# A mixture of experts on one core: seven wide products per pair, four of them summed in one PSUM bank, two weight sums made by adding DMAs

## What is computed

```python
h = relu(einsum('bi,eio->beo', x, eW1) + eb1)       # 512 x 1024 by 1024 x 1024, 8 experts
h = relu(einsum('beh,eho->beo', h, eW2) + eb2)      # to 512
expert_out = einsum('beh,eho->beo', h, eW3) + eb3   # to 256
gates = softmax(einsum('bi,tie->bte', x, gW) + gb, axis=-1)      # 2 tasks
tin = einsum('bte,bed->btd', gates, expert_out)
th = relu(einsum('btd,tdh->bth', tin, tW1) + tb1)
th = relu(einsum('bth,tho->bto', th, tW2) + tb2)
out = sigmoid(einsum('bth,tho->bto', th, tW3) + tb3)[..., 0]
```

## Time and profile before

| | us |
|---|---|
| median of three runs (579.86 to 580.24) | 580.05 |
| the profiled execution | 580.12 |
| its span, first to last instruction | 578.5 |
| TensorE busy | 572.7 |
| VectorE busy | 462.6 |
| ScalarE busy | 265.3 |
| GpSimd busy | 44.1 |

### The profile page before, as it was taken

One profiled execution on the slowest core, in us unless ns is written; L12 is line 12 of the kernel. 1 busy time (PEld: TensorE's weight loads), 2 busy tenths in 40 slices (PEclk: granted clock), 3 DMA queues, 4 the chain that ended last, 5 costly groups with the idle time before them and its releaser, 6 DMA issues.

```text
span 578.5 us, 9216 instructions
## 1 busy us (share of the span) xinstructions
PE 572.7 (99%) x3315; PEld 501.7 (87%) x3315; DVE 462.6 (80%) x590; ACT 265.3 (46%) x336; POOL 44.1 (8%) x46
## 2 busy tenths in 40 slices
PE   8999999999999999999999999999999999999998
PEld 5788899988999889988999889988999889998776
DVE  6955489985998769895898859987699859988492
ACT  3545274524545164333654255351654346533553
POOL 0000100030000300012000300003000210004000
PEclk9999999999999999999999999999999999999999
DMA  8340622243131514215223422415131241235000
GB/s 311 137 145 1 229 101 74 76 173 116 73 117 64 188 66 145 73 60 230 73 73 108 161 93 73 145 36 220 42 137 73 97 193 73 73 131 167 29 0 2
DMA packets 23277, 63.27 MB, mean 109 GB/s; under 512 B 1617, under 2 KB 6865, under 8 KB 19682
## 3 DMA queue, kind: packets, MB, share of 16 engines
q1 hardware_dynamic: 21906, 58.64, 28.3%
q0 software_dynamic: 1216, 4.23, 2.0%
q10 hardware_dynamic: 144, 0.26, 0.1%
HBM read 63.08 MB, written 0.04 MB: 109 GB/s over the span
## 4 chain that ended last, share of the span: by engine, by line
PE 96%; DMA 1%; ACT 1%; DVE 1%; issue 0%; SPq 0%; ACTq 0%
PE psum L280 25%; PE psum L282 25%; PE psum L281 25%; PE psum L425 13%; PE psum L427 7%; DMA w_raw<-eW_first 1%; DVE w_lo L787 0%; PE psum L487 0%; ACT w_hi L742 0%; ACT w_hi L586 0%; ACT scratch L777 0%; PE psum L572 0%; SPq L300 0%; DVE scratch L1079 0%; ACT h_hi L680 0%
## 5 line engine op out<-in xcount | busy, mean ns | idle before, releaser
L280 PE MATMUL psum<-h_hi,w_hi 128*128 128x512 f32 (+1 forms) x340 | 131.6, 387 | 0.8 <-DVE h_lo L798 0.8
L282 PE MATMUL psum<-h_hi,w_lo 128*128 128x512 f32 (+1 forms) x340 | 131.6, 387 | 0.0
L281 PE MATMUL psum<-h_lo,w_hi 128*128 128x512 f32 (+1 forms) x340 | 131.6, 387 | 0.0
L787 DVE TENSOR_TENSOR w_lo<-w_raw,w_hi 128x1024 fp32r<-128x1024 f32 (+1 forms) x79 | 111.2, 1426 | 3.2 <-ACT w_hi L742 1.7
L798 DVE SCALAR_TENSOR_TENSOR h_lo<-scratch,h_hi 128x512 fp32r<-128x512 f32 (+1 forms) x68 | 61.7, 909 | 50.1 <-ACT scratch L681 37.8
L282 PE MATMUL psum<-t_both,w_lo 128*128 128x256 f32 x336 | 95.1, 283 | 0.0
L281 PE MATMUL psum<-t_both,w_hi 128*128 128x256 f32 x336 | 95.0, 283 | 0.0
L280 PE MATMUL psum<-t_both,w_hi 128*128 128x256 f32 x336 | 95.0, 283 | 0.0
L627 ACT ACTIVATE w_hi<-w_raw 128x1536 fp32r<-128x1536 f32 x28 | 41.8, 1494 | 90.4 <-PE psum L282 46.2
L280 PEld LDWEIGHTS psum<-h_hi,w_hi 128*128 128x128 f32 x340 | 63.9, 188 | 14.2 <-DVE h_lo L798 1.2
L282 PEld LDWEIGHTS psum<-h_hi,w_lo 128*128 128x128 f32 x340 | 63.8, 188 | 13.0
(11 more groups left out here) (101 smaller groups left out, 798.6 us busy)
## 6 DMA issues: line engine op xcount, KB each, us to landing
w_raw<-eW_pairs SPq DMA_DIRECT2D x28, 1024.0 KB, 4.8
w_raw<-eW SPq DMA_DIRECT2D x40, 512.0 KB, 3.7
scratch<-gates_dram POOLq DMA_DIRECT2D x8, 512.0 KB, 3.9
w_raw<-eW_first SPq DMA_DIRECT2D x7, 512.0 KB, 6.3
w_raw<-tW SPq DMA_DIRECT2D x4, 512.0 KB, 3.4
scratch<-xT SPq DMA_DIRECT2D x7, 256.0 KB, 6.2
w_raw<-eW_first SPq DMA_DIRECT2D x2, 256.0 KB, 4.0
scratch<-xT ACTq DMA_DIRECT2D x1, 256.0 KB, 3.4
```

Of the source, the lines that this page charges most:

```text
L280: pe.matmul(bank, weights_hi, moving_hi, start=first, stop=False)
L281: pe.matmul(bank, weights_hi, moving_lo, start=False, stop=False)
L282: return pe.matmul(bank, weights_lo, moving_hi, start=False, stop=last)
L787: dve.tensor_tensor(wide(w_lo, slots), raw, wide(w_hi, slots).bitcast(F32), ALU.subtract).then_inc(slot_ready, 1)
```

## The change

All seven products are wide, in the order P1, P2, P5, P6, P4 of the pair before, P3, P7; P4 of the last pair stands between layer 3 and layer 2. P1, P6, P7 and P4 of a pair are summed one upon the other in one bank (N_BANK); ScalarE reads the bank after P1 (`n1_take`), after P6 (`n2_take`) and after P4 (`c21_take`), VectorE after P7 (`c22_sum`). P5 and P3 share another bank (Q_BANK), read by ScalarE between them (`p5_take`) and by VectorE behind P3 (`c12_sum`). P2 has a bank of its own. TensorE waits for each such reading before it adds to the bank. VectorE folds the halves (`upper_fold`, `lower_fold`, `c21_fold`). The weight blocks of a pair lie in the order A22, A11, A12, A21; their sums and those of x have other signs. S2 and S4 are made on VectorE as before. S1 and S3 are made by transfers from GpSimd's queue that add a block from DRAM to one that SP has loaded: per pair, SP loads 768 KB of blocks, 256 KB for S3 and 256 KB of A22, and GpSimd adds 256 KB twice. The splits of a pair are four groups: G1 (three slots), G2 (one), G3 (two), G4 (one). GpSimd's loop is unrolled. The four gated outputs are `gate_output(e, n)` at places of their own. Buffers in SBUF are laid out anew and the units of W3, W2 and the tower weights are others.

```diff
-PRODUCTS = [((0, 10), True, "x", 1, 0),
-            ((4, 14), False, "x", 0, 0),
...
+N_BANK, Q_BANK, P2_BANK = [2, 6, 3, 2], [0, 1, 0, 1], [3, 4, 5, 4]
+PRODUCTS = {"P1": (N_BANK, "x", 0, 0, True, False), "P2": (P2_BANK, "x", 1, 0, True, True), "P5": (Q_BANK, "t", 0, 0, True, False),
+            "P6": (N_BANK, "t", 1, 1, False, False), "P4": (N_BANK, "t", 1, 0, False, True), "P3": (Q_BANK, "x", 1, 1, False, True),
+            "P7": (N_BANK, "t", 0, 1, False, False)}
+SPLIT_ORDER = [("G1", 0), ("G2", 0), ("G3", 0), ("G1", 1), ("G4", 0), ("G2", 1), ("G3", 1), ("G4", 1),
+               ("G1", 2), ("G2", 2), ("G3", 2), ("G1", 3), ("G2", 3), ("G4", 2), ("G3", 3), ("W3",), ("G4", 3),
+               ("W2", 0), ("W2", 1), ("W2", 2), ("W2", 3)]
...
# SP, per expert
+                sp.wait_ge(slot_ready, splits(e) - 2)
+                load_blocks(e, 0)
+                load_a22(e, 0)
+                sp.wait_ge(slot_ready, splits(e))
+                load_blocks(e, 1)
+                load_a22(e, 1)
+                for i in range(2):
+                    sp.wait_ge(slot_ready, split(e, "G3", i))
+                    load_blocks(e, i + 2)
+                    sp.wait_ge(slot_ready, split(e, "G4", i))
+                    load_a22(e, i + 2)
...
# TensorE
...
+            def product(e, p, i):
...
+                for kk in range(KK):
+                    pe.matmul(whole, weights(w_hi, kk), moving(kk), start=(starts and kk == 0), stop=False,
+                              skip_group_check=True)
+                for kk in range(KK):
+                    mm = pe.matmul(whole[:, 0, :], weights(w_lo, kk), moving(kk)[:, 0, :], start=False,
+                                   stop=(ends and kk == KK - 1), skip_group_check=True)
+                mm.then_inc(slot_used, 1)
             def pair(e, i):
...
+                product(e, "P1", i)
+                if i >= 2:
+                    pe.wait_ge(upper_done, PAIRS * (e - 1) + i - 1)
+                product(e, "P2", i)
...
+                product(e, "P5", i)
+                pe.wait_ge(n1_taken, PAIRS * (e - 1) + i + 1)
+                pe.wait_ge(slot_ready, split(e, "G2", i))
+                product(e, "P6", i)
+                if i > 0:
+                    last_product(e, i - 1)
+                pe.wait_ge(p5_taken, PAIRS * (e - 1) + i + 1)
+                pe.wait_ge(slot_ready, split(e, "G3", i))
+                product(e, "P3", i)
+                pe.wait_ge(n2_taken, PAIRS * (e - 1) + i + 1)
+                product(e, "P7", i)
+            def last_product(e, i):
+                pe.wait_ge(lower_summed, PAIRS * (e - 1) + i + 1)
+                pe.wait_ge(slot_ready, split(e, "G4", i))
+                product(e, "P4", i)
...
                 layer3(e, last=False)
+                last_product(e, PAIRS - 1)
                 layer2(e)
...
# ScalarE, start and end of the loop's list
+                g1_hi(e, 1)
+                g4_hi(e, 0)
+                n1_take(e, 0)
+                take_hidden2(e, 3)
+                p5_take(e, 0)
+                g2_hi(e, 1)
+                n2_take(e, 0)
...
+                pair_h1(e, 1)
+                g3_hi(e, 3)
+                w3_split(e)
+                n1_take(e, 3)
+                g4_hi(e, 3)
+                p5_take(e, 3)
+                n2_take(e, 3)
+                c21_take(e, 2)
+                pair_h1(e, 2)
+                w2_hi(e, 0)
+                w2_hi(e, 1)
+                c21_take(e, 3)
+                w2_hi(e, 2)
+                pair_h1(e, 3)
+                w2_hi(e, 3)
...
# VectorE
+            def c22_sum(e, i):
...
+                dve.tensor_tensor(lower[:], lower[:], halved(banks[N_BANK[i]]), ALU.subtract).then_inc(lower_summed, 1)
+            def lower_fold(e, i):
...
+                dve.scalar_tensor_tensor(quarter[:, 3, :], lower[:, 0, :], prm_of("b1", e * K2 + MG + i),
+                                         lower[:, 1, :], ALU.add, ALU.add).then_inc(lower_done, 1)
...
# VectorE, from the splits of pair 3 to the end of the loop's list (the splits of W2 stood ahead of gate_expert)
+                c12_sum(e, 2)
+                c22_sum(e, 2)
+                pair_h1_lo(e, 1)
+                upper_fold(e, 2)
+                g2_lo(e, 3)
+                g4_lo(e, 2)
+                lower_fold(e, 2)
+                g3_lo(e, 3)
+                c11_sum(e, 3)
                 w3_lo(e)
+                c21_fold(e, 2)
+                g4_lo(e, 3)
+                c12_sum(e, 3)
+                pair_h1_lo(e, 2)
+                upper_fold(e, 3)
+                c22_sum(e, 3)
+                gate_output(e, 0)
+                gate_output(e, 1)
+                lower_fold(e, 3)
                 w2_lo(e, 0)
+                gate_output(e, 2)
                 w2_lo(e, 1)
+                c21_fold(e, 3)
                 w2_lo(e, 2)
+                gate_output(e, 3)
+                pair_h1_lo(e, 3)
                 w2_lo(e, 3)
-                gate_expert(e)
...
# GpSimd
-            with pool.Fori(1, E) as e:
+            for e in range(1, E):
+                for i in range(PAIRS):
+                    count = 2 * (e - 1) + i // 2 + 1
+                    pool.wait_ge(blocks_landed[i % 2], count * DMA)
+                    pool.dma_start(raw_block(i, A21), blocks_dram(e, i, A22), accum_op=ALU.add) \
+                        .then_inc(s1_summed[i % 2], DMA)
+                    pool.wait_ge(s3_landed[i % 2], count * DMA)
+                    pool.dma_start(sums[:, S3[i % 2], :], blocks_dram(e, i, A21), accum_op=ALU.add) \
+                        .then_inc(s3_summed[i % 2], DMA)
                 for o in range(OUT3):
```

More of the change, by code:

```diff
@@ L85 @@
 BANK_FINAL = [4, 0, 1]
+W3_UNIT, W2_UNIT = 1, [0, 3, 2, 3]
+LAST_W3_UNIT, TOWER_UNIT = 1, [0, 2, 3, 1]
+PER_UNIT = [([W3_UNIT] + W2_UNIT).count(u) for u in range(UNITS)]
 TAIL_ADDS = [0, 1, 2, 3]
@@ L99, with used, free_early, split @@
 NSMALL = _at
[L102 to L111, removed]
+def used(e, product):
+    return USED0 + (e - 1) * USED + AT[product] + 1
+def free_early(e, u):
+    return USED0 + (e - 1) * USED - 6 + u
 def splits(e):
     return SPLITS0 + (e - 1) * SPLITS
-def pair_slots(i, at, n):
-    first = (NP * i + at) % RING
-    return slice(first, first + n)
+def split(e, *what):
+    return splits(e) + SPLIT_ORDER.index(what) + 1
+def slot_of(product):
+    return USER[product] % RING
 def moe_towers(nc, xT, eW1_first, eW1_pairs, eW2, eW3, tW1, tW2, small, out):
@@ L314, in _ @@
-            with sp.Fori(1, E) as e:
[L315 to L331, removed]
@@ L467, in layer3 @@
                 else:
-                    pe.wait_ge(slot_ready, splits(done) + 3 * PAIRS + 1)
+                    pe.wait_ge(slot_ready, split(done, "W3"))
                     pe.wait_ge(h2_ready, K3 * done)
-                    pe.wait_ge(combined, PAIRS * (done - 1) + 3)
+                    pe.wait_ge(upper_done, PAIRS * done - 1)
                 for i, (k, o) in enumerate(by_bank(range(K3), OUT3)):
+                    if not last and i == K3:
+                        pe.wait_ge(upper_done, PAIRS * done)
                     if last and i < K3:
@@ new lines, in g1_hi, with g2_hi @@
+            def g1_hi(e, i):
+                act.wait_ge(s1_summed[i % 2], (2 * (e - 1) + i // 2 + 1) * DMA)
+                wait_slots(e, USER["P1", i], 3)
+                first = slot_of(("P1", i))
+                act.activation(wide(slice(first, first + 3)), raw_block(i, A11, 3), ACT.Copy).then_inc(slot_hi, 1)
+            def g2_hi(e, i):
+                act.wait_ge(summed, 2 * PAIRS * (e - 1) + 2 * i + 1)
+                wait_slots(e, USER["P6", i], 1)
+                act.activation(w_hi[:, slot_of(("P6", i)), :], sums[:, S2, :], ACT.Copy).then_inc(slot_hi, 1)
@@ new lines, in g3_hi @@
+            def g3_hi(e, i):
+                act.wait_ge(s3_summed[i % 2], (2 * (e - 1) + i // 2 + 1) * DMA)
+                act.wait_ge(summed, 2 * PAIRS * (e - 1) + 2 * i + 2)
+                wait_slots(e, min(USER["P3", i], USER["P7", i]), 2)
+                first = min(USER["P3", i], USER["P7", i]) % RING
+                at = min(S4, S3[i % 2])
+                act.activation(wide(slice(first, first + 2)), sums[:, at:at + 2, :].rearrange("p s w -> p (s w)"),
+                               ACT.Copy).then_inc(slot_hi, 1)
@@ new lines, in _ @@
+                upper_fold(e, 0)
+                sum2(e, 2)
+                sum4(e, 2)
+                c22_sum(e, 0)
+                lower_fold(e, 0)
+                g4_lo(e, 1)
+                g1_lo(e, 2)
+                c11_sum(e, 1)
+                c21_fold(e, 0)
+                c12_sum(e, 1)
+                g2_lo(e, 2)
+                pair_h1_lo(e, 0)
+                upper_fold(e, 1)
+                g3_lo(e, 2)
+                c22_sum(e, 1)
+                lower_fold(e, 1)
+                c11_sum(e, 2)
```

536 lines of the change are left out of this document (252 added, 284 removed).

## The result

The changed kernel takes 594.33 us (median of 4 runs, 592.22 to 595.82), the kernel before 580.01 beside it: a ratio of 1.0244, 95% interval 1.0212 to 1.0275. The forecast was 583.2 us, with a range up to 584.8: the sign was right, and the size was missed by 11 us, beyond the range. The profiled execution took 594.49 us, its span 592.7.

A forecast was written before the change was run, and what follows sets the result against it. TensorE was taken as the bound, busy 572.7 of 578.5 us. From 580.12, 4.4 saved by wide products and 7.7 added by layer 2 stalls gave 583.4, forecast as 583.2; range 575.3 to 584.8, main case 581.5 to 584.6.

The forecast's parts named there:

- What the change removes from TensorE: Products in the expert loop: wide takes 1.40 us, narrow 1.44; four per pair become wide over 28 pairs, 4.4 us saved.
- Engine work: Stretch of pairs: VectorE falls to about 33 of 39.2 us, ScalarE rises to about 27; neither becomes the bound.
- The new waits inside a pair: TensorE's waits for PSUM readings at P3, P7 and P6: all met, 0 taken, up to 0.5 us per expert otherwise.
- the slacks of 0.4 us: Pair 0: the readings before P3 and P7 finish 0.4 us before those products are due.
- Where a stall goes in: Start of layer 2: VectorE's w2_lo(0) takes turns with GpSimd's adds; 1.1 us late per expert, 7.7 us in all.
- The accumulating transfers: GpSimd's adding transfers for S1 and S3: 3.9 us each, ends 2.5 and 7.8, landing within slack; 0 taken.
- the 7.8 us end: Adding transfer's upper landing time, twice 3.9 since the destination is read too; costs at most a microsecond, once.
- The rival on late transfers: Adding transfers land late, beyond pair 3's 5 us slack; slower, 589.7 us or more at an 11 us landing; chance 0.06.
- The sum: Whole kernel: 580.12 - 4.4 + 7.7 = 583.4, against the median 583.3; forecast 583.2 us, slower.
- the short waits' upper end: Rival: short waits at P3 or P7 of pair 0 bite, 0.1 to 0.5 us per expert, 576.4 to 578.8; chance 0.09.

The follow-up runs named there:

- Experiment 8: Changed kernel with W2's first split ahead of gate 0, next expert's pair 0 loaded earlier, and S1, S3 made by VectorE additions instead of adding transfers: 606.16 us.
- Experiment 3: Changed kernel with W2's first split ahead of gate 0 and no adding transfers (unsummed blocks stand in for S1 and S3): 575.81 us.
- Experiment 4: Changed kernel with lower_fold(3) and W2's first split swapped, the split now first, both still behind gates 0 and 1: 596.47 us.
- experiment 2: Changed kernel without the adding transfers; unsummed blocks stand in for S1 and S3, and waits go to the loads alone: 584.61 us.
- experiment 9: Changed kernel with W2's first split ahead of gate 0, pair 0 loaded earlier, and pair 1's load held until pair 0's sums landed: 616.68 us, single run.

## Why the prediction was right, and where it failed

- **What the change removes from TensorE**: right. 1.403 us for each product, and 575.81 without waits against 575.7.
- **Engine work**: right. VectorE 33.42 (33 said), ScalarE 25.70 (27 said) in a stretch of pairs, neither of them the bound. Experiment 8 suggests how near VectorE is to it: by its estimate, the 1.22 us per pair that I listed as taken off VectorE keep it under TensorE. One step of the working was loose: 1280 more elements at 0.69 us for 512 are 1.7 us per pair, not 1.4; the trace has 0.95 ((25.70 - 21.92) / 4).
- **The new waits inside a pair**: right, 0. Experiment 3, with both causes removed, has no such wait, so even the slacks of 0.4 us held. In the kernel after, the late sum used up the one at P3 of pair 0 and held P3 by another 0.14 us. The wait at P6 of pair 0 stood on no list: only P6 of pair 3 was worked out.
- **Where a stall goes in**: right, in mechanism and nearly in size. Seven waits of 1.0 at layer 2, `w_lo` 2.31 long (2.2 said) and ready 5.0 us behind the first bank of layer 3 (5.05 said), `lower_fold` held: the TENSOR_TENSOR's row did speak for the SCALAR_TENSOR_TENSOR. The Trainium skill (SBUF — State Buffer, Who interferes with whom) says that a VectorE instruction with two SBUF inputs contends with a GpSimd instruction that reads SBUF. The trace agrees, with 1.08 us for 0.48. 7 x 1.16 = 8.1 us in the trace for the 7.7 forecast; removal gave 9.5, 1.2 of it at P6. Experiment 4 confirms the order of the turns.
- **The accumulating transfers**: this step failed. It said "I take 3.9", the landing of GpSimd's plain load of 512 KB, gave pair 0 a slack of "4 to 5", and so took 0 for the whole term, where the runs show 9.7 us (experiment 2). The slack was right: 5 us between 8.7 us for both transfers and the moment needed. The two prices were not. The load took 6.7 us where 4.8 was the median over all pairs, and the addition 8.2, above even the upper end of 7.8. Together they are 6.2 us late in expert 3, 1.1 more than the slack. In the six experts the waits are 0.9 to 1.8 us, and with what they bring along 10.1 us in the stretches of pairs. Three mistakes in one term: a median taken over all places for a place that is the most crowded (the block loads, the gates' load and the next pair's load are issued within 6.3 us there, 192.59 to 198.84, and the DMA share then reaches 0.95, where I argued from a mean over the span); bytes taken for the price, where the runs show it in packets and engine time (1.9 times that of a copy); and the 7.8 us end costed as "at most a microsecond, once", though pair 0 comes in every expert. The rival on late transfers had the mechanism and 0.06 of the chance, and looked for it at pair 3. The price would have been too low by a page's fit as well. The Trainium skill (DMA: Bandwidth & Descriptors, Anatomy of one DMA — SWDGE (gpsimd) path) gives about 2.0 us and the bytes over 436e3, an estimate of 2.6 us for 256 KB; the trace disagrees, with 4.1 as the median of copies and 5.3 of additions.
- **The sum**: 583.2 forecast. With the measured term of the late sum, 9.7 by experiment 2, it would have been 592.9; most of the rest to 594.3 is in the turns (9.5 by removal, 7.7 forecast), less the 0.7 by which the two don't add. Two slips carry nothing: the working's own sum is 583.3, not 583.2, and 0.5 us in seven experts would make the short waits' upper end 579.2, not 578.8.

## What to carry to other kernels

A sum that is made by a second transfer is a chain of two landings, and it has to be costed at its worst place, the first tile behind a phase of other loads, and with every engine list that it starts late: TensorE's wait will name the last reader, not the transfer. Moving one instruction out of the reach of GpSimd's additions, and one load a piece earlier, each brought back over 8 us with no work saved. Where an engine's list has a piece of work on its critical side, read what stands ahead of it in the list, and not only when its own inputs are ready.

## What was not expected of the hardware

- A transfer that adds 256 KB into SBUF took 5.3 to 6.0 us in the median for 4.1 to 4.2 of a copy, held the DMA engines 1.9 times as long, and its issue on GpSimd 0.87 to 1.12 us for 0.54.
- A wait of TensorE costs more than the length in its row, even where the granted clock stays at 1.00: the 13 waits of the kernel after are 14.4 us, and their removal gave 18.5. The rest counts as busy time, 573.4 against 568.7 in experiment 3, some 0.35 us per wait. The rows show where it lies. The last matmul's row goes on beyond the next one's due start, so layer 2 of expert 2 is 1.16 late by a wait of 1.00. The four matmuls behind a wait at P6 are 1.19 long for 1.09. And P3 behind such a wait is late by another 0.14 and is 1.19 long as well.
- Behind longer waits the clock sometimes falls, and the same length of wait does not always do it: behind 1.78 us in experiment 4 the next 3 us were at 0.68 once and at 1.00 once, behind 1.85 us in experiment 8 at 0.57, behind 1.86 at 1.00, behind 4.18 in experiment 9 at 0.50. Behind the six waits at P6 of the kernel after, 0.88 to 1.78 us, it stayed at 1.00. What decides it, these runs leave open.
